# Row maxima of the first layer by DMA instead of TensorE and ScalarE, in a two-layer cross-attention kernel

## The reference

```
layer 0: q = x Wq; scores = q k^T / 4, over text tokens (77) and IP tokens (the other 435), a softmax for each
         out = softmax(text) v + softmax(ip) v_ip; x = out Wo + bo + x
layer 1: softmax over 508 text tokens, whose probabilities also give a semantic query (probs x context),
         compared with 4 IP tokens; a second softmax over those 4, masked; the same output product and residual
```

## Time and profile before

| | |
|---|---|
| median of 3 timed runs | 1718.63 us (1717.26 to 1721.88) |
| profiled execution | 1711.14 us |
| its span, first to last instruction | 1709.3 us |
| TensorE busy | 1585.5 us (93%) |
| VectorE busy | 1272.5 us (74%) |
| ScalarE busy | 1113.4 us (65%) |
| GpSimd busy | 459.7 us (27%) |
| DMA queue of SyncE | 76.77 MB, 14.6% of 16 engines |

### The profile page before, as it was taken

One profiled execution on the slowest core, in us unless ns is written; L12 is line 12 of the kernel. 1 busy time (PEld: TensorE's weight loads), 2 busy tenths in 40 slices (PEclk: granted clock), 3 DMA queues, 4 the chain that ended last, 5 costly groups with the idle time before them and its releaser, 6 DMA issues.

```text
span 1709.3 us, 32278 instructions
## 1 busy us (share of the span) xinstructions
PE 1585.5 (93%) x8608; PEld 1212.0 (71%) x8608; DVE 1272.5 (74%) x3548; ACT 1113.4 (65%) x2323; POOL 459.7 (27%) x1233
## 2 busy tenths in 40 slices
PE   7888999999988899999998899999999889999993
PEld 3554489999455459999855537999965544899991
DVE  2797378887788538888778935888877983688875
ACT  1797367775399537777449925777727982677760
POOL 0343023332044213223115402333303440233320
PEclk9999999999999999999999999999999999999997
DMA  9010310010411221000131022000031103000000
GB/s 312 24 37 14 111 58 21 18 34 2 123 38 36 60 83 37 18 18 30 40 97 37 28 69 92 19 18 18 25 111 35 37 19 111 15 19 19 22 17 15
DMA packets 47715, 82.81 MB, mean 48 GB/s; under 512 B 4868, under 2 KB 12308, under 8 KB 47640
## 3 DMA queue, kind: packets, MB, share of 16 engines
q1 hardware_dynamic: 44968, 76.77, 14.6%
q10 hardware_dynamic: 2672, 5.13, 0.8%
HBM read 41.49 MB, written 34.10 MB: 44 GB/s over the span
## 4 chain that ended last, share of the span: by engine, by line
PE 78%; ACT 12%; issue 5%; DVE 2%; DMA 1%; SPq 1%; ACTq 0%; POOL 0%; DVEq 0%
PE ps_w L938 45%; PE ps_t L938 12%; PE ps_s L938 12%; PE ps_b L938 7%; ACT probsT_high L522 5%; ACT probsT L530 5%; PE ps_m L938 2%; DVE row_max L729 1%; DMA q_slots<-out_all 1%; ACT probs L541 1%; ACT q_slots L515 1%; DMA q_slots<-probsT_low 1%; SPq L350 0%; ACT probs L618 0%; POOL probsT_low L433 0%
## 5 line engine op out<-in xcount | busy, mean ns | idle before, releaser
L522 ACT ACTIVATE probsT_high<-ps_t 128x512 fp32r<-128x512 f32 x640 | 382.6, 598 | 118.1 <-PE ps_t L938 114.2
L714 DVE TENSOR_TENSOR probsT_low<-probsT,probsT_high 128x512 fp32r<-128x512 f32 x560 | 394.7, 705 | 77.8 <-ACT probsT L530 68.7
L938 PE MATMUL ps_w<-gram,probsT_high 128*128 128x416 f32 (+2 forms) x1280 | 387.5, 314 | 0.0
L530 ACT ACTIVATE probsT<-ps_t 128x512 f32<-128x512 f32 x640 | 384.3, 600 | 0.0
L938 PE MATMUL ps_w<-gram_low,probsT_high 128*128 128x384 f32 (+2 forms) x1280 | 351.5, 303 | 0.0
L453 POOL TENSOR_SCALAR exp_bias<-row_max 128x1 f32<-128x1 f32 x320 | 128.0, 400 | 689.3 <-DVE row_max L772 689.3
L558 ACT ACTIVATE probs<-ps_s,exp_bias 128x508 f32<-128x508 f32 x320 | 220.3, 689 | 123.8 <-POOL exp_bias L453 79.9
L938 PE MATMUL ps_t<-q_slots,k_slots 98*128 98x512 f32 x640 | 259.7, 424 | 0.9
L938 PEld LDWEIGHTS ps_w<-gram_low,probsT_high 128*128 128x128 f32 (+1 forms) x1280 | 242.3, 189 | 11.0
L938 PEld LDWEIGHTS ps_w<-gram,probsT_high 128*128 128x128 f32 (+1 forms) x1280 | 240.8, 188 | 11.5
L938 PE MATMUL ps_s<-k_slots,q_slots 96*128 96x512 f32 x640 | 238.0, 414 | 10.2 <-DMA q_slots<-out_all 4.0
(11 more groups left out here) (166 smaller groups left out, 2024.5 us busy)
## 6 DMA issues: line engine op xcount, KB each, us to landing
q_slots<-parts_q SPq DMA_DIRECT2D x128, 96.0 KB
k_slots<-parts_k SPq DMA_DIRECT2D x128, 96.0 KB
parts_k<-probsT_high SPq DMA_DIRECT2D x16, 512.0 KB, 4.8
parts_k<-probsT_high SPq DMA_DIRECT2D x24, 256.0 KB, 4.2
parts_q<-probsT_low SPq DMA_DIRECT2D x8, 512.0 KB, 4.3
parts_q<-x_sb SPq DMA_DIRECT2D x8, 512.0 KB, 4.6
k_slots<-probsT_high SPq DMA_DIRECT2D x24, 128.0 KB, 3.9
parts_q<-probsT_low SPq DMA_DIRECT2D x12, 256.0 KB, 4.0
```

The lines of the kernel that those rows point to most:

```text
L522: nc.scalar.activation(probsT_high[1 - par][:, t, :], ps_t[:, t % 2, :], ACT.Exp, scale=SCALE)
L530: nc.scalar.activation(probsT[:, t, :], ps_t[:, t % 2, :], ACT.Exp, scale=SCALE).then_inc(pt_block[l], 1)
L714: nc.vector.tensor_tensor(probsT_low[1 - par][:, t, :], probsT[:, t, :], probsT_high[1 - par][:, t, :].bitcast(F32), ALU.subtract).then_in ...
L938: return nc.tensor.matmul(out, lhsT, rhs, start=start, stop=stop)
```

## The change

In layer 0, `head_maxT` and `shift` go. VectorE writes the maxima as `row_max[p, kind, chunk]`, and SyncE copies them with two DMAs for each head, one for each kind, straight into rows 96 and 97 of the q slot, once the maxima of the second half are there (`shift` of SyncE, semaphores `rows_in`). The copy puts the value of partition p and chunk c at column 4 p + c, so a chunk of scores now takes the queries 4 p + c as its weights, every fourth column of the slot. TensorE waits for these DMAs ahead of transposed block 0, and VectorE ahead of the next maxima that go into the same buffer.

The scores run half a head further ahead: step n computes the second half of head n+2 first, and the first half of head n+3 where the second half of n+2 was. The q and k slots become one tensor and the scratch tensors one for each layer, so that one DMA of 192 KB fills a head's slot, in both layers. The outputs of the batch before are stored after the slot loads and rows of layer 0. Layer 1 keeps `head_maxT` and `shift`.

```diff
-SLOT_LOADS = 2 * 16
+SLOT_LOADS = 16
+SHIFTS = SHIFT_ROWS * 16
...
-        scratch = {n: nc.dram_tensor(f"parts_{n}", [3, TURNS, D, SLOTS, S], F32, kind="Internal").ap()
-                   for n in ("k0", "q0", "k1", "q1")}
+        scratch_of = [nc.dram_tensor(f"parts{l}", [3, TURNS, D, SLOTS, 2, S], F32, kind="Internal").ap() for l in range(2)]
+        scratch = {f"{n}{l}": scratch_of[l][:, :, :, :, i, :] for l in range(2) for i, n in enumerate("qk")}
...
+        slots = sb("slots", [ALL_ROWS, SLOTS, 2, S], F32R)
+        q_slots, k_slots = slots[:, :, 0, :], slots[:, :, 1, :]
...
+        def rows_loaded(eng, b, k, turn):
+
+            eng.wait_ge(rows_in[k % SLOTS], SHIFTS * (TURNS * b + turn + k // SLOTS + 1))
...
-                for slot, src in ((q_slot[k], scratch[f"q{l}"]), (k_slot[k], scratch[f"k{l}"])):
-                    sp.dma_start(slot[0:SCORE_ROWS, :].bitcast(F32), src[:, turn, :, k, :])\
-                        .then_inc(slots_in[l][k], 16)
+                sp.dma_start(slots[0:SCORE_ROWS, k, :, :].bitcast(F32), scratch_of[l][:, turn, :, k, :, :]).then_inc(slots_in[l][k], 16)
...
-                if l == 0 and b is not FIRST:
-                    store_outputs(b)
+                if l == 0:
+                    shift(batch, 0, 0)
+                    shift(batch, 1, 1)
                 for name in names:
                     sp.wait_ge(stored[name], STORES * (batch + 1))
                 sp.sem_inc(passed, 1)
                 with sp.Fori(0, TURNS - 1) as turn:
                     for k in range(SLOTS):
                         load_slots(batch, l, turn + 1, k)
+                        if l == 0:
+                            shift(batch, SLOTS * turn + k + 2, (k + 2) % SLOTS)
+                if l == 0:
+                    for k in range(2, SLOTS):
+                        shift(batch, HEADS - SLOTS + k, k)
+                if l == 0 and b is not FIRST:
+                    store_outputs(b)
+
+            def shift(b, n, k):
+
+                sp.wait_ge(max_half, 2 * (HEADS * b + n + 1) + CREDIT)
+                for r in range(SHIFT_ROWS):
+                    sp.dma_start(q_slots[SHIFT_ROW + r:SHIFT_ROW + r + 1, k, :].bitcast(F32),
+                                 row_max[0][k % 2][:, r, :].bitcast(F32)).then_inc(rows_in[k], 16)
...
-                if scores:
-                    shift(b, 0, n + 1, k + 1)
...
-                if scores and (use or transposed or last is FIRST):
-                    maxima0(b, n + 2, 0, par)
+                first = not use and not transposed
+                if first and last is FIRST:
+                    maxima0(b, 0, 0, 0)
+                if scores:
+                    maxima0(b, n + 2, 1, par)
+                if first:
+                    maxima0(b, 1, 0, 1)
...
-                if scores:
-                    maxima0(b, n + 2, 1, par)
+                if scores_next and not first:
+                    rows_loaded(dve, b, k + 1, turn)
+                    maxima0(b, n + 3, 0, 1 - par)
...
+                q = q_slot[slot][0:FULL_ROWS, :].rearrange("r (p c) -> r c p", c=SC)[:, c, :] if l == 0 else \
+                    q_slot[slot][0:FULL_ROWS, P * c:P * c + P]
+                return mm(out, q, k_slot[slot][0:FULL_ROWS, :], True, True)
...
+                if first:
+                    scores_half(2, 0)
+                    values0(last)
                 if scores:
-                    scores_half(0)
-                if first:
-                    values0(last)
+                    scores_half(2, 1)
...
                 if transposed:
+                    rows_loaded(pe, b, k + 1, turn)
                     scoresT_of(0, g, k, 0)
...
-                if scores:
-                    scores_half(1)
+                if scores_next and not first:
+                    scores_half(3, 0)
...
-                if scores:
-                    pe.wait_ge(max_half, 2 * (g + 3) + CREDIT)
-                    head_maxT(0, par)
+                if first:
+                    scores_half(3, 0)
```

More of the change, by code:

```diff
@@ L218, in build @@
         low_last = sem("low_last")
-        maxT_done = [sem(f"maxT_done{l}") for l in range(2)]
-        shift_in = [sem(f"shift_in{l}") for l in range(2)]
+        maxT_done = sem("maxT_done")
+        shift_in = sem("shift_in")
+        rows_in = [sem(f"rows_in{i}") for i in range(SLOTS)]
         gram_high = sem("gram_high")
@@ L267, in fill0 @@
         def fill0(step, batch, b=FIRST):
-            step(batch, -2, SLOTS - 2, -1, False, False, True, b)
-            step(batch, -1, SLOTS - 1, -1, False, True, True, b)
+            step(batch, -2, SLOTS - 2, -1, False, False, True, True, b)
+            step(batch, -1, SLOTS - 1, -1, False, True, True, True, b)
+        def rows_loaded(eng, b, k, turn):
+            eng.wait_ge(rows_in[k % SLOTS], SHIFTS * (TURNS * b + turn + k // SLOTS + 1))
         def run_heads0(step, eng, b):
@@ L410, in _, with step0 @@
                                     pattern=[[-1, P]], channel_multiplier=1).then_inc(built, 1)
-            def step0(b, n, k, turn, use, transposed, scores, last=FIRST):
+            def step0(b, n, k, turn, use, transposed, scores, scores_next, last=FIRST):
                 par = k % 2
@@ L563, in step1 @@
                 if transposed:
-                    shift(b, 1, n, k)
+                    shift(b, n, k)
                 if second:
@@ L727, in maxima0, with step0 @@
                 dve.wait_ge(s_half, 2 * (HEADS * b + head) + half + 1)
-                nc.vector.tensor_reduce(out=row_max[0][par][:, cs, 0:1], in_=ps_s[:, :, 0:TEXT0], axis=AX.X, op=ALU.max)
-                nc.vector.tensor_reduce(out=row_max[0][par][:, cs, SHIFT_ROWS - 1:SHIFT_ROWS], in_=ps_s[:, :, TEXT0:T],
+                nc.vector.tensor_reduce(out=row_max[0][par][:, 0, cs], in_=ps_s[:, :, 0:TEXT0], axis=AX.X, op=ALU.max)
+                nc.vector.tensor_reduce(out=row_max[0][par][:, 1, cs], in_=ps_s[:, :, TEXT0:T],
                                         axis=AX.X, op=ALU.max).then_inc(max_half, 1)
-            def step0(b, n, k, turn, use, transposed, scores, last=FIRST):
+            def step0(b, n, k, turn, use, transposed, scores, scores_next, last=FIRST):
                 par = k % 2
                 outputs = transposed and not use and last is not FIRST
-                if scores and (use or transposed or last is FIRST):
-                    maxima0(b, n + 2, 0, par)
+                first = not use and not transposed
[5 more added lines that the diff above has]
+                    maxima0(b, 1, 0, 1)
                 if outputs:
@@ L976, in scoresT_of, with wait_slot, head_maxT, step0 @@
             def scoresT_of(l, g, k, t):
-                if t == 0:
-                    pe.wait_ge(shift_in[l], g + 2)
+                if t == 0 and l == 1:
+                    pe.wait_ge(shift_in, g + 2)
                 pe.wait_ge(pt_block[l], TB * (g + 1) + t - 1 + CREDIT1)
                 scoresT_block((k + 1) % SLOTS, t, ps_t[:, t % 2, :]).then_inc(st_block[l], 1)
-            def wait_slot(b, l, n, k, turn):
-                pe.wait_ge(slots_in[l][(k + 2) % SLOTS], HEAD_LOADS * b + SLOT_LOADS * (turn + (k + 2) // SLOTS) + CREDIT)
-            def head_maxT(l, par):
+            def wait_slot(b, l, k, turn, ahead):
+                pe.wait_ge(slots_in[l][(k + ahead) % SLOTS], HEAD_LOADS * b + SLOT_LOADS * (turn + (k + ahead) // SLOTS) + CREDIT)
+            def head_maxT(par):
                 for c in range(SC):
-                    rows = row_max[l][par][:, c, :]
-                    last = mm(ps_m[0:SHIFT_ROWS, P * c:P * c + P], rows if l == 0 else rows.to_broadcast([P, SHIFT_ROWS]),
+                    last = mm(ps_m[0:SHIFT_ROWS, P * c:P * c + P], row_max[1][par][:, c, :].to_broadcast([P, SHIFT_ROWS]),
                               ident_r[:, :], True, True)
-                last.then_inc(maxT_done[l], 1)
-            def step0(b, n, k, turn, use, transposed, scores, last=FIRST):
+                last.then_inc(maxT_done, 1)
+            def step0(b, n, k, turn, use, transposed, scores, scores_next, last=FIRST):
                 par = k % 2
                 g = HEADS * b + n
-                def scores_half(half):
-                    if half == 0:
-                        wait_slot(b, 0, n, k, turn)
-                    pe.wait_ge(max_half, 2 * (g + 2) + half + CREDIT)
+                def scores_half(ahead, half):
+                    if half == 0 and ahead == 3:
+                        wait_slot(b, 0, k, turn, 3)
+                    pe.wait_ge(max_half, 2 * (g + ahead) + half + CREDIT)
                     for i in range(2):
-                        last = scores_chunk((k + 2) % SLOTS, 2 * half + i, ps_s[:, i, :])
+                        last = scores_chunk(0, (k + ahead) % SLOTS, 2 * half + i, ps_s[:, i, :])
                     last.then_inc(s_half, 1)
```

26 lines of the change are left out of this document (12 added, 14 removed).

## The result

| | before | after |
|---|---|---|
| median | 1717.95 us (1713.71 to 1721.88) | 1777.49 us (1773.41 to 1791.84) |
| ratio, 95% interval | | 1.036 [1.033, 1.039] |
| span of the profiled execution | 1709.3 us | 1775.4 us |
| mean granted clock | 0.991 | 0.961 |

What follows compares the result with a forecast made beforehand. The first layer was taken as bound by a 5.45 us loop per head through ScalarE and TensorE, shift included. 72 x (5.45 - 4.95) = 36, less 3 for fills, is 33 us: from 1718.6 to 1686 us, range 1673 to 1714.

Steps and rivals of the forecast that it cites:

- L: Time from the end of a head's maxima to both rows landed: taken as 3.1 us, between 2.6 and 4.8.
- the row by DMA: SyncE's two row DMAs per head in the first layer: hidden, with 0.3 us to spare, at 4.95 us a step.
- nothing is won or lost there: Merging two slot loads of 96 KB into one of 192 KB frees one issue; slots are wanted over a step later.
- So neither blocks the other: SyncE's order: slot load and rows don't hold each other up, as the load's condition is met ahead of the maxima.
- The rival of late rows: TensorE waits ahead of the first transposed block: 21 us slower, 1739; chance 0.13, shared with loads beyond 0.45 us.
- 2T = L + 6.47: Loop closed by the row DMAs over two steps of period T: at T = 4.95, L may be 3.43 us.
- The loop without the shift: First layer's head step: ScalarE and TensorE fall from 5.45 to 4.70 us, VectorE needs 4.84, so 4.95 with waits.
- Strided weights: Score chunks' weight loads: 0.10 us more per load, 0 to 0.22 us in the loop; low end taken.
- The rival that took them for the bound: Strided loads doubled to 0.38 us make the step 5.30 us: 8 us gained, 1711; chance 0.08.
- The fills: Start of each batch's first layer: 0.7 us net for three batches, 1 for the first; 3 in all, bounds 0 and 8.
- most of it comes back: In the fills y starts some 2 us later, mostly regained by work and waits missing later, leaving 0.7 us net.
- The sum: 72 x (5.45 - 4.95) = 36, less 3 for the fills: 33 us gained.

Runs made afterwards that it cites:

- rows_first: The changed kernel with SyncE issuing the two row DMAs ahead of the single slot load: 1787.63 us, ratio 1.039.
- two_loads: The changed kernel with q and k of a slot loaded by one DMA of 96 KB each, as before the change: 1738.71 us, ratio 1.012.
- short_maxima: three_loads_plain_weights with the first layer's second maximum taken over 179 tokens instead of 435: 1671.87 us in a single timed run.
- three_loads_plain_weights: three_loads with each chunk's queries taken as 128 neighbouring columns instead of every fourth: 1685.61 us, ratio 0.984.
- lead_by_engines: three_loads with plain weights and rows made by TensorE's four matmuls and ScalarE's copy, no row DMA, half-head lead kept: 1723.35 us, ratio 1.004.
- three_loads: The changed kernel with each slot load cut into three DMAs of 64 KB: 1697.57 us, ratio 0.988.
- half_after_output: three_loads_plain_weights with the second half of head 1's scores put behind the first part of y in the fills of batches 2 to 4: 1680.32 us, ratio 0.977.
- own_maxima: three_loads, strided weights kept, with the fill of half_after_output: 1690.89 us, ratio 0.985.
- before_strided: The kernel before the change with every fourth column taken as a chunk's weights, in both layers: 1722.46 us, ratio 1.001.

## Why the prediction was wrong

**What failed: L.** The step that fell is "the row by DMA", the term L, which the prediction put at 3.1 us with 4.8 as the most and break-even at 4.43. Measured it is 5.3 us in the steps shown (4.8 to 6.1 over the batch). What was mis-sized in it is the slot load ahead of the rows: the prediction named the rule that the rows land no sooner than that load, and put into it the 3.9 us of the earlier trace rows, which are the landings of 128 KB copies. No row showed a slot load's landing, neither of 96 KB nor of the merged 192 KB. The merging was noted ("nothing is won or lost there") and not priced. The new load takes 5.5 us in the chain of rows_first and 6.0 in the median of the kernel after; issued at 99.62, it gives the landing of the rows at 106.02 less the 0.35 us by which they follow it.

**"So neither blocks the other" held for the kernel after.** In every head of it the rows are issued as soon as their maxima are done. It would have failed with the two loads of before, whose issues hold the rows back for 0.7 us (two_loads).

**The rival of late rows was right in place and sign, short in price.** It had 1739 us at L = 4.8. Its formula, 2T = L + 6.47, can be checked on each pair of steps, from the end of one maxima with a late row to the end of the next:

| from | two steps, us | L | L + 6.47 | excess | clock granted after the landing |
|---|---|---|---|---|---|
| 74.58 | 12.63 | 6.13 | 12.60 | 0.0 | 1.00 |
| 87.21 | 13.50 | 5.64 | 12.11 | 1.4 | 0.54 |
| 100.71 | 12.91 | 5.31 | 11.78 | 1.1 | 0.56 |
| 113.62 | 12.06 | 5.58 | 12.05 | 0.0 | 1.00 |
| 125.68 | 12.69 | 4.91 | 11.38 | 1.3 | 0.55 |
| 138.37 | 13.56 | 5.74 | 12.21 | 1.4 | 0.57 |

With the true L the formula holds where TensorE restarts at the upper level of its clock, and is 1.1 to 1.4 us short where it restarts at the lower one. The true L in the formula makes 6.0 us a step of the 6.4 measured in this table, and the rest stands where the clock is low. The prediction had no term for the clock.

**The loop without the shift held.** 4.70 us for ScalarE and TensorE (short_maxima: 4.70), 4.84 for VectorE and 0.08 beside it (three_loads_plain_weights: 4.92), the row's way through TensorE and ScalarE as the thing that goes (lead_by_engines: 5.45 with it). With quick loads L is no longer than was taken: the DMAs land in 1.9 us, and the step is 5.0 where 4.95 was forecast.

**Strided weights: the size was right, the cover was not.** 0.13 us for each load instead of 0.10, and 0.09 us a step instead of zero, within the bound of 0.22; the words "as VectorE's 4.84 covers most of it" were wrong by these 6 us or more. The rival that took them for the bound has fallen.

**The fills were too cheap.** Forecast 0.7 us for each of three and 1 for the first. Measured in three_loads: 20.7, 22.1 and 22.3 us where it was 18.2, so 2.5 to 4.1 more, and in the first batch the first move of `outT0` comes at 66.15 where it was at 59.27, 6.9 us later. TensorE's wait ahead of `y` was seen rightly ("some 2 us"); the sentence "most of it comes back" was the wrong one, as half_after_output and own_maxima show, where moving the half away from there brings most of it back. Of the 6.9 us, 2.2 lie ahead of the first scores (37.54 against 35.39). From there to the first move it takes 23.9 us before, 28.6 in three_loads and 27.6 in lead_by_engines, which has no row by DMA: so most of that loss comes with the lead of half a head. What in it costs this, no run took apart.

**The sum, had L held.** In the profiled executions of before and three_loads the moves of `outT0` from a batch's first to its last take 102.4 and 93.9 us, 33.9 us less over four batches. The three fills take back 10.5, the first batch 6.9, and the second layer and the end 4.0: 12.5 us, the difference of the spans (1709.3 and 1696.8). By the medians three_loads gained 1719.43 - 1697.57 = 21.9, since the profiled execution of before was a quick one, 7.5 us under its median. Where 33 was forecast, the mechanism was good for two thirds of its price by the medians and less by the profiles, and one DMA's shape turned it into a loss.

## What to carry to other kernels

A DMA that joins a loop pays for what stands ahead of it on its queue: work out its landing as the landing of the transfer before it, and take that one's time in its new size and shape, never from the row of another transfer that goes to the same tile. Look at the outermost dimension of both sides of every load; 3 x 16 rows as one dimension of 48, or as three DMAs, took 2.9 or 2.1 us where 3 x 16 took 5.5. And before you blame a queue's order, look up when the instruction behind the wait was free to go: the chain of waits led through a slot load here, and the rows behind it had been held by their own maxima.

## What the runs showed of the hardware

- 192 KB from DRAM to 48 partitions: 5.5 us to land (rows_first; 6.0 in the median of the kernel after) and 0.78 us to issue with a source that begins with a dimension of 3; 2.9 us and 0.32 us with 48 rows in one dimension. The share of the 16 DMA engines at work was 0.18 and 0.72. The issue time moves with the shape too: three DMAs of 64 KB are issued in 1.36 us together.
- A pair of DMAs of 128 pieces of 16 bytes each, from 128 partitions into one, lands in 1.8 to 3.1 us if nothing slow is ahead of them, in 4.3 to 5.6 behind the single load, 0.35 us after it in the median.
- Weights with 16 bytes from one column to the next: 320 ns for 128 float32 columns, 188 for neighbouring ones; behind back-to-back matmuls the difference costs nothing (before_strided).
- The granted clock was 0.90 between 100 and 150 us in the kernel after, where TensorE stood still for a late row some eight times in the first batch, 1.0 to 2.0 us each; in three_loads, without these waits, it was 1.00 in the same window. It fell at waits of 1.16, 1.25, 1.59 and 1.96 us, and stayed at 1.00 at others of 1.02, 1.11, 1.22 and 1.59.
